# An attention kernel's row maxima are computed 22 tasks ahead instead of 24, and the first head group's loads are issued later

## What is computed

```python
xn = _layernorm(x, axis=-1)
qkv = (xn @ W_qkv + b_qkv).reshape(B, T, 3, H, Dh).transpose(2, 0, 3, 1, 4)
q = q * cos + rotate_half(q) * sin
k = k * cos + rotate_half(k) * sin
attn = jax.nn.softmax(jnp.einsum('bhqd,bhkd->bhqk', q, k) * scale, axis=-1)
out = jnp.einsum('bhqk,bhkd->bhqd', attn, v)
...
weights, idx = _gate(xn, w_gate)
routed = jnp.einsum('tef,ehf,te->th', g * u, w2_e, combine)
x = x + (out @ W_out + b_out) + routed + shared
```

## Time and profile before

| | us |
|---|---|
| median of 3 runs | 1224.29 |
| lowest and highest | 1221.29, 1224.77 |
| the profiled execution | 1225.57 |
| its span | 1224.1 |

### The profile page before, as it was taken

One profiled execution on the slowest core, in us unless ns is written; L12 is line 12 of the kernel. 1 busy time (PEld: TensorE's weight loads), 2 busy tenths in 40 slices (PEclk: granted clock), 3 DMA queues, 4 the chain that ended last, 5 costly groups with the idle time before them and its releaser, 6 DMA issues. The chain is left out here.

```text
span 1224.1 us, 27785 instructions
## 1 busy us (share of the span) xinstructions
PE 1152.4 (94%) x8309; PEld 583.8 (48%) x8311; DVE 959.7 (78%) x1451; ACT 751.4 (61%) x1568; POOL 578.4 (47%) x861
## 2 busy tenths in 40 slices
PE   4997749999999999999999999998999999998998
PEld 2554423333333333333333333333788787885665
DVE  6574568899999999999999999980555555556888
ACT  4664412788888888888888888888333333331000
POOL 6998756463556563231323232332566666661000
PEclk9998865899999999999999999999999999999999
DMA  6466544445445442433234322411677667655765
GB/s 221 156 209 211 178 136 136 188 109 159 111 124 150 123 131 85 110 99 101 74 100 105 98 84 85 105 35 52 210 225 232 200 208 213 193 166 180 238 220 174
DMA packets 127288, 181.74 MB, mean 148 GB/s; under 512 B 41441, under 2 KB 88929, under 8 KB 125282
## 3 DMA queue, kind: packets, MB, share of 16 engines
q1 hardware_dynamic: 111842, 138.55, 38.7%
q0 software_dynamic: 15360, 42.04, 9.9%
HBM read 99.71 MB, written 80.81 MB: 147 GB/s over the span
## 5 line engine op out<-in xcount | busy, mean ns | idle before, releaser
L1049 DVE TENSOR_REDUCE mx<-pm 128x1 f32<-128x1024 f32 x512 | 621.4, 1222 | 24.8 <-PE pm L1099 24.3
L1023 ACT ACTIVATE pr<-pst 128x512 f32<-128x512 f32 x1024 | 556.7, 596 | 80.5 <-PE pst L1110 28.5
L1099 PE MATMUL pm<-kt,qt 48*128 48x512 f32 x1024 | 387.2, 461 | 12.0 <-PEq L141 6.8
L1110 PE MATMUL pst<-qt,kt 50*128 50x512 f32 x1024 | 379.0, 450 | 0.0
L1122 PE MATMUL po<-pr,vt 128*17 128x256 f32 x4096 | 323.7, 388 | 9.9 <-ACT osb L1033 9.6
L1099 PEld LDWEIGHTS pm<-kt,qt 48*128 48x128 f32 x1024 | 157.5, 193 | 236.9 <-DVE mx L1049 173.4
L1275 POOL DMA_INDIRECT s_y<-ys_c,slot_c x144 | 139.5, 969 | 85.6 <-issue 46.4
L1122 PEld LDWEIGHTS po<-pr,vt 128*17 128x17 f32 x4096 | 69.0, 95 | 199.5 <-issue 110.9
L1110 PEld LDWEIGHTS pst<-qt,kt 50*128 50x128 f32 x1024 | 153.5, 187 | 11.7 <-ACT pr L1023 10.9
L951 POOL DMA_INDIRECT s_xg<-p_rows,p_slot x128 | 125.1, 978 | 56.0 <-issue 30.1
L1355 PE MATMUL pd<-w13s,xt_c 128*128 x576 | 149.4, 382 | 0.1
(11 more groups left out here) (187 smaller groups left out, 1168.4 us busy)
## 6 DMA issues: line engine op xcount, KB each, us to landing
xg<-s_xg SPq DMA_DIRECT2D x144, 128.5 KB
yg<-s_y SPq DMA_DIRECT2D x32, 512.0 KB, 3.8
s_q<-stg SPq DMA_DIRECT2D x32, 256.0 KB
s_k<-stg SPq DMA_DIRECT2D x32, 256.0 KB
kt<-s_k SPq DMA_DIRECT2D x32, 256.0 KB
qt<-s_q SPq DMA_DIRECT2D x64, 128.0 KB
s_o<-osb SPq DMA_DIRECT2D x32, 256.0 KB, 7.2
w13s<-w SPq DMA_DIRECT2D x1, 4608.0 KB, 14.7
```

Source lines behind the costliest of these rows:

```text
L1023: nc.scalar.activation(pr[:, (k % 2) * 4 + ORDER[i], :], pst[bank(gg, k, i)][:, :], ACT.Exp, scale=SCALE).then_inc(exp_ok, 1)
L1049: nc.vector.tensor_reduce(mx[:, half, col:col + 1], pm[slot][:, :, :].rearrange("p a n -> p (a n)"), AX.X, ALU.max).then_inc(mx_free, 1)
L1099: mm = pe.matmul(pm[slot][:, kk, :], qt[buf][rows, half, pair, qi * P:(qi + 1) * P], kt[buf][rows, pair, kk * 512:(kk + 1) * 512], start=T ...
L1110: pe.matmul(pst[bank(buf, k, i)][:, :], kt[buf][rows, pair, kc * P:(kc + 1) * P], qt[buf][rows, half, pair, :], start=True, stop=True)\
```

## The change

Two things. AHEAD goes from 24 to 22. With it SWITCH goes from 4 to 5, ROWS1 from 4 to 5 and ROWS0 from 12 to 13: 22 maxima are computed ahead of the first quad, next group's begin with quad 5, and the rows are turned in quads 5 and 13, the sixth quad of each half group. The waits of VectorE for GpSimd's split and of TensorE for next group's keys and queries stand at SWITCH and SWITCH + 8 and move with it. The last group has maxima in quads 0 to 4. The quads that need the rows stay (8 and 0), and so does use 18 for the first rows.

The 13 loads of the first group are no longer issued at k = 16 to 28 of SP's loop but at k = 30, 32, 34 and 36, behind the stores of `store_xt` and `store_v` of that step; those with the same purpose are issued together.

```diff
             def first_loads(k, t, b):
-                n = k - 2 * TPB
+                n = k - 3 * TPB
                 if n == 0:
                     for i in range(2):
                         sp.wait_ge(st_out[i], STORES * 16)
                     for i in range(TPB):
                         sp.wait_ge(v_out[i], 16)
-                if n in (0, 2):
-                    load_keys(sp, s_k, first["kt"][0], 0, first["qk_in"], (n // 2,))
-                if n in (4, 6):
-                    load_queries(sp, s_q, first["qt"], 0, 0, first["qk_in"], (n // 2 - 2,))
-                if n in (8, 10):
-                    load_queries(sp, s_q, first["qt"], 1, 0, first["late_in"], (n // 2 - 4,))
-                if n == 12:
+                    load_keys(sp, s_k, first["kt"][0], 0, first["qk_in"])
+                if n == 2:
+                    load_queries(sp, s_q, first["qt"], 0, 0, first["qk_in"])
+                if n == 4:
+                    load_queries(sp, s_q, first["qt"], 1, 0, first["late_in"])
+                if n == 6:
                     load_values(sp, s_v, first["vt"], 0, 0, first["v_in"])
...
-                for lag, part in ((0, store_xn), (TURN, store_xt), (PROJ, store_v), (0, first_loads), (BACK, store_parts)):
+                for lag, part in ((0, store_xn), (TURN, store_xt), (PROJ, store_v), (BACK, first_loads), (BACK, store_parts)):
...
-AHEAD = 24
+AHEAD = 22
 SWITCH = (32 - AHEAD) // 2
 ROWS1, ROWS0 = SWITCH, SWITCH + 8
```

## The result

| | before | after |
|---|---|---|
| median us | 1224.14 | 1269.35 |
| lowest and highest us, 4 runs each | 1221.29, 1224.77 | 1267.37, 1280.66 |
| profiled execution, its span us | 1225.57, 1224.1 | 1271.21, 1269.4 |

The ratio is 1.0395, with a 95% interval of 1.034 to 1.0449. The change makes the kernel 45 us slower. The forecast was 1250 us with a range up to 1266 us; the sign was right, and the size lies outside the range.

What follows compares the result with a forecast made beforehand. The prediction took VectorE's maxima (2.44 us per quad) to bound the attention stage and GpSimd to pace stage A. Its sum, 1225.57 - 8.3 + 0 + 33.9 = 1251.2 us, gave a forecast of 1250 us, range 1234 to 1266 us.

Steps and rivals of the forecast that it cites:

- Waits of the loop: Attention loop: handing over turned rows needs 5.09 us but keeps 3.96; TensorE waits 1.13 us, 30 times, 33.9 us.
- The estimate by the fixed cost of about 2.0 us: Same hand-overs, from the page alone: need 2.0 + 1.33 + 2.0 = 5.3 us, 1.4 us per half group, 41 us.
- Stage A: Stage ahead of attention, 0 to 173 us: 13 loads leave SP's queue ahead of the last stores, gain 8.3 us.
- these stores are issued about 8.3 us earlier: Stage A: without 8.34 us of load issues, SP issues the stores ScalarE waits on last about 8.3 us earlier.
- The upper bound, 13.9 us: Stage A: largest gain, if every GpSimd wait for ScalarE from 60 to 172 us went.
- Landing of the late loads at nothing: End of stage A: the moved loads land under the routing tail, cost 0.
- first score 31.6 us after the stage's start as before: Start of attention stage B: first score 31.6 us after the stage's start, unchanged, with TensorE idle ahead of it.
- third rival: Start of stage B: the first queries and keys land too late, up to 8 us lost, 1258 us; chance 0.13.
- 22 ahead at nothing: Before stage B's first quad: two maxima fewer gain 0, at most 2.44 us, as the first score waits for rows.
- fourth rival: Attention loop: more DMA contention, 21 us more, 1271 us, or a colder TensorE with a lower clock; chance 0.09.
- Rival 1: Attention loop: the waits are absorbed, only stage A's gain stays, 1216 us; chance 0.06.
- rival 2: Attention loop: waits half absorbed or hand-overs short, 0.47 us each, 14 us in all, 1230 us; chance 0.12.

Runs made afterwards that it cites:

- e1: The first group's loads late as in the changed kernel, but AHEAD back at 24, against the kernel before: 1216.49 us, ratio 0.995.

## Why the prediction was wrong, by its own steps

**Waits of the loop: right, also in the pieces.** The sum had 30 waits of 1.13 us, 33.9 us; the trace has 33.5 us, and none in the last hand-over, as said. The mean pieces over half groups 1 to 30, in the order of the prediction: 1.73, 1.35 and 1.94 us, 5.02 us in all and 5.07 us to the start of the score, against 1.69 + 1.33 + 2.07 = 5.09; the room is 3.95 us against 3.96. Reading a need of three pieces from rows of before, where nothing yet waited, and subtracting the room was enough. The estimate by the fixed cost of about 2.0 us that the Trainium skill gives in "DMA: Bandwidth & Descriptors", "Anatomy of one DMA", was 41 us. That section measures DMAs that GpSimd issues, which the prediction didn't say, and these are issued by SP: here the store's first piece took 1.73 us and the landing of the loads 1.94 us, both under it.

**Stage A: the term was too small, 8.3 against 13.7 us.** The step that failed is "these stores are issued about 8.3 us earlier". They are issued 13.7 us earlier: the last eight begin at 131.92 instead of 145.64. Up to there the loads that are gone make 8.3 us, and the issues that stay are 4.7 us shorter in all; of the eight stores of half a batch, for instance, the two pairs for `s_k` took 2.04 and 2.51 us instead of 3.92 and 3.40. Little is left for SP's waits. SP's queue before, then after:

```profile
123.30 3.92 SPq L487 DMA_DIRECT2D s_k<-stg  x2
...
145.64 1.27 SPq L487 DMA_DIRECT2D s_q<-stg  x2
```

```profile
116.42 2.04 SPq L486 DMA_DIRECT2D s_k<-stg  x2
...
131.92 1.26 SPq L486 DMA_DIRECT2D s_q<-stg  x2
```

The prediction had the stretching in mind, and used it only as a reason against the gain. The upper bound, 13.9 us from GpSimd's idle time, held.

**Landing of the late loads at nothing: right for stage B's first maximum, wrong for the first rows.** TensorE's first matmul for a maximum starts 0.47 us after the stage's first load issue, and the trace puts that start down to the landing of the queries; before it was 0.04 us. So the landing just fits. But "first score 31.6 us after the stage's start as before" failed: 38.4 us. I had looked at the loads as transfers that must land, and not at the queue that they leave full behind them. Issues of up to 2.26 us for two stood in the earlier trace rows. The third rival came nearest with its 8 us, though by another way: not the queries of the first maximum, but the store of the first rows was late. The chance of 0.13 was too low for something that the e1 run has with certainty.

**22 ahead at nothing: right.** With the 22 alone (e2_ahead_only) the first score comes 31.62 us after the stage's first loads, against 31.60 before, and TensorE waits 2.11 us for the rows ahead of it, near the 2.4 us that were predicted.

**The clock: left out of the sum, and this alone takes it out of the range.** The fourth rival said "gaps of 1 us don't do it there", from a window with 1.14 us of work in 2 us, which holds a single gap of 0.86 us. That was right for 1 us: the 24 waits of up to 1.29 us in the changed kernel had no fall. The step that failed is the use of a mean: waits of 1.13 us in the mean have a spread, 0.32 to 2.62 us in this run, and the prediction itself had 2.78 us as the longest. Six of the 30 were 1.59 us and longer, four of them were followed by a clock of 0.50, and those four cost 24.8 us, against 33.5 us for all the waits themselves. With 1225.57 - 13.7 + 6.8 - 2.7 + 32.5 + 24.8 - 2.4 = 1270.9 us the sum meets the profiled 1271.21. Without the falls it would have been 1246 us, well inside the range: the two errors of the start (5.4 us too little gained, 6.8 us not charged) nearly cancel. So had no clock fallen, the forecast would have been met in part by luck.

How sure is the link between waits and falls? On the first chip, the two kernels with waits around 1.1 us had 12 waits of 1.57 us and longer, and 9 of them had a fall; 48 shorter ones had none; the kernel before and the late loads alone, without such waits, had no fall in the loop; and with waits of 2.9 to 4.5 us each half group had one. What tells the 3 from the 9 is open. On the other chips it falls without a wait for rows too, mostly behind idle stretches of TensorE of over 1.0 us beside GpSimd's sends. So a late row is one way to an idle TensorE and not the only one.

**Rival 1 (absorbed)** fell, as did rival 2: a wait passes fully into the interval of the half groups. This holds for a loop in which VectorE and TensorE are in step at full clock. On a chip of the second sort VectorE has slack (with the late loads alone it waits 180.2 us for TensorE's `pm` from 200 to 1035 us, against 23.5 us from 200 to 840 us on the first chip), and the same edit costs a quarter as much.

## What to carry to other kernels

Take a hand-over apart into issue, wait and landing, and compare it with the room; this gives the mean wait. Then look at the longest ones, since a TensorE that waits for more than some 1.5 us in a dense loop can lose its clock for another 3 to 20 us (9 of 12 such waits did on the first chip), and a mean of 1.1 us hides that. Issues taken out of a full queue give back more than their own time, and the same issues put close ahead of the next stage make its first small store late (5.36 us here): order that queue by who waits.

## What the runs showed of the hardware

- The granted clock fell from 1.00 to 0.50 after waits of 1.57 to 2.77 us in a loop where TensorE was otherwise busy, stayed low for 13.7 to 20.5 us of full work in the changed kernel (3.4 to 13.7 us in the one with 22 ahead alone), and came back by itself.
- One kernel (late loads, no waits for rows) has a clock of 1.00 over 240 to 840 us on one chip and 0.82 on another, 1216.49 and 1385.73 us. Its first score is at 198.0 and 196.6 us, so the stage ahead takes the same on both. Of the five chips of the experiments four were of the slower sort.
- On those four TensorE stands idle for over 1.0 us beside GpSimd's indirect sends, 21 to 25 times in the loop of the kernels without late rows, and most falls of the clock come behind that. With the sends of 16 half groups put later these took 383 to 391 us instead of 422, and the clock was low for 72 to 92 us instead of 167.
- Two loads of 8 KB landed 1.90 us behind their issue with GpSimd's indirect sends beside them, and 1.55 us with the sends put later (means over 16 half groups).
- Two DMA issues of the same store on SP's queue took 3.92 us with the 13 loads issued among the stores and 2.04 us without them; 8.3 us of issues taken away gave back 13.7 us.
